# Attention with a planned order on TensorE: new planner constants, a longer lead, larger rings and masks in fp32r

## The chip, the cores and the metric

The kernel runs on one core of one Trainium2 chip. The time is that of the whole kernel on the device, in microseconds (us), as the median of three runs. A core has TensorE (PE, matmuls and weight loads), VectorE (DVE), ScalarE (ACT), GpSimd (POOL) and SyncE (SP, which issues the DMAs here). Each runs its own list of instructions in order, and they wait for each other by semaphores. Matmuls write to eight banks of PSUM, 512 fp32 columns each; DVE and ACT read them from there.

## What is computed

A transformer layer on x of shape (1, 4096, 256): a modulated layer norm, causal attention with 16 heads of 16 dimensions and rotary positions, a residual with a gate, a second norm, a dense layer, eight experts in fixed slices, a last dense layer, a second gated residual. The change touches the attention alone:

```python
scores = jnp.einsum('bhqd,bhkd->bhqk', q, k) * scale
mask = jnp.where(kpos > qpos, jnp.float32(-jnp.inf), jnp.float32(0.0))
scores = scores + mask[None, None]
attn = jax.nn.softmax(scores.astype(jnp.float32), axis=-1).astype(q.dtype)
out = jnp.einsum('bhqk,bhkd->bhqd', attn, v)
```

## The kernel before

The kernel has a projection stage (to about 140 us), the attention stage (`attend_block`, to about 1737 us) and a feed-forward stage (`feed`, to the end). Attention is cut into 32 tasks (`TASKS`): four quads of four heads, and in each quad eight chunks of 512 queries. A task with chunk c (0 to 7) sees c + 1 chunks of keys. `STEPS` are the blocks of 128 keys of each task, 4(c + 1) of them; the last four of a task lie on the diagonal, have 512, 384, 256 and 128 columns, and need the causal mask.

Scores are computed twice. The first time, `most` (lines 831 to 851), they stand with queries as rows, and DVE takes their maximum per row (line 940). `UNITS` lists this work, 8(c + 1) pairs of matmuls per task. When a task is through, DVE joins its maxima (line 946), POOL splits them into two fp32r parts (lines 979, 981), PE turns them (`turn`, line 859), ACT copies them out (line 917), and SP spreads them as extra rows of the queries (`spread`, line 764, by DMA from m_rows to q_aug). The second time, `scores` (line 817), the scores stand with keys as rows, the maximum is subtracted by those extra rows, and ACT takes the exponential (line 908). Then `values` (line 879) multiplies them with v into PSUM bank 3, in plain fp32. At a task's end ACT copies the result out (line 924), PE turns it (`norm`, line 867), and DVE divides by the row sums (lines 954, 956).

One `score` or `most` is a pair of fp32r matmuls that run side by side in the upper and lower 64 rows of the array (r = 0, 1), into two of the seven free banks. On the diagonal four small matmuls of 128 columns add the mask to the two banks (lines 825 and 849): id_h times later_h, both bf16, in two halves of 64 rows each.

What PE, ACT, DVE and SP do in which order is written out by `plan()` before the kernel is built. It keeps a clock for PE, ACT and DVE, and when each bank is free; at each turn it lists what could come next on PE (a score, a most, a turn, a norm, a values), reckons when each could begin (`begin_at`), and takes the one of least cost. The cost weighs how far ACT's or DVE's clock is ahead, biases, and PACE times the wait of PE. The constants below `plan()` say what each thing takes in its model. The model sets the order alone; on the chip semaphores decide when things run.

Limits on the order: a `most` of task n may be chosen only while n <= main + LEAD, where main is the task whose scores are next; its queries must have a slot in q_aug (QRING slots, freed when the scores of task n - QRING are done); its keys must have one of the KRING slots of k_aug (line 747; keys k beyond the first KRING wait until the scores of the last task of the quad of key k - KRING are done). Scores run at most PROBS = 4 blocks ahead of values.

SP's queue at the start of attention: keys 0 and queries 0, the two masks, a constant, queries 1 and keys 1, then 2 x KRING small writes of ones into the key slots (line 779), then the loads of the other slots, and only then what `SP_ORDER` lists: spreads, and reloads of queries and keys. The first `score` waits for the first spread, and for all writes of ones.

Of the kernel before, what the change touches and what calls it, by code (L numbers as in the profile page):

```python
# [25 lines left out]
P = 128  # L26
# [46 lines left out]
PV_BANK = 3  # L73
KRING = 12
QRING = 5
PROBS = 4
LEAD = 3


def step_width(s):  # L80
    n, kb = STEPS[s]
    return CW - P * max(kb - TILES * TASKS[n][1], 0)
# [16 lines left out]
def plan():  # L99

    pe_order, act_order, dve_order, sp_order = [], [], [], []
    pe = act = dve = 0.0
    wide = False
    free = {b: 0.0 for b in BANKS}
# [10 lines left out]

    def begin_at(ready, to_wide):
        if wide == to_wide and ready > pe - RELOAD:
            return max(pe + RELOAD, ready)
        return max(pe + (TO_VALUES if to_wide else FROM_VALUES if wide else 0), ready)

# [24 lines left out]
    while pair < pairs or val < len(STEPS) or at < len(UNITS) or turn or norm:  # L145
        choices = []
        main = STEPS[pair // JP][0] if pair < pairs else len(TASKS)
        if pair < pairs:
            s = pair // JP
            if main in rows and s - PROBS < val:  # L150
                banks, ready = take(2)
                begins = begin_at(max(ready, rows[main]), False)
                choices.append((act - begins + PACE * max(begins - pe, 0), "score", begins, banks))
        if at < len(UNITS):
            n = UNITS[at][0]
            if n <= main + LEAD and not (turn and late_nm is not None) and (n < QRING or n - QRING in main_end):
                banks, ready = take(2)
                begins = begin_at(max(ready, main_end[n - QRING] + LOAD_NS if n >= QRING else 0.0), False)
                choices.append((dve - begins + MOST_BIAS + PACE * max(begins - pe, 0), "most", begins, banks))
        for kind, small in (("turn", turn), ("norm", norm)):  # L160
            if small:
                banks, ready = take(1)
                begins = begin_at(max(ready, small[0]), False)
                choices.append((SMALL_BIAS + PACE * max(begins - pe, 0), kind, begins, banks))
        if val < pair // JP and not (norm and LAST[STEPS[val][0]] == val):
            begins = begin_at(max(exp_end[val], pv_free if STEPS[val][1] == 0 else 0.0), True)
            choices.append((VALUES_BIAS - VALUES_STEP * (pair // JP - val) + (VALUES_AGAIN if wide else 0)
                            + PACE * max(begins - pe, 0), "values", begins, None))
        _, kind, begins, banks = min(choices, key=lambda c: c[0])
        after = read_by(banks) if banks else None  # L170
        if kind == "score":
# [9 lines left out]
            if b == JP - 1 and LAST[main] == s:  # L181
# [3 lines left out]
                if s in LAST_OF_QUAD:  # L185
                    g = LAST_OF_QUAD.index(s)
                    for k in range(CHUNKS * g + KRING, min(CHUNKS * (g + 1) + KRING, CHUNKS * QUADS)):
                        sp_order.append((act, "keys", k))
            pair, pe, wide = pair + 1, begins + max(w * PE_COLUMN + PE_FIXED, PE_LEAST) + masks, False
        elif kind == "most":  # L190
# [9 lines left out]
            if at == LAST_UNIT[n]:  # L200
                if n == 0 or n == len(TASKS) - 1:
                    maxima_of(n)
                else:
                    late_nm = n
            at, pe, wide = at + 1, begins + max(w * PE_COLUMN + PE_FIXED, PE_LEAST) + masks, False
        elif kind == "turn":
            pe_order.append(("turn", turn[1], None, banks, after))
            pe, wide = begins + TURN_NS, False
            on_act(("turn", turn[1], None, banks[0]), pe + PE_TO_ACT, CW * ACT_COLUMN + ACT_FIXED, banks[0])
            rows[turn[1]] = act + SPREAD_NS  # L210
            sp_order.append((act, "spread", turn[1]))
            turn = None
        elif kind == "norm":
            pe_order.append(("norm", norm[1], None, banks, after))
            pe, wide = begins + TURN_NS, False
            on_dve(("norm", norm[1], None, banks[0]), pe + PE_TO_DVE, NORM_NS, banks[0])
            norm = None
        else:
            n = STEPS[val][0]
            pe_order.append(("values", val, None, None, None))  # L220
            pe, wide = begins + step_width(val) * PV_COLUMN, True
            pv_end[val] = pe
            if val == LAST[n]:
                on_act(("out", n, None, PV_BANK), pe + PE_TO_ACT, CW * ACT_COLUMN + ACT_FIXED, None)
                pv_free = act + ACT_TO_PE
                norm = (pv_free, n)
            val += 1
# [3 lines left out]
PE_COLUMN, PE_FIXED, PE_LEAST = 1 / 2.4, 22, 110  # L231
PV_COLUMN = 853 / 512
TO_VALUES, FROM_VALUES, RELOAD = 214, 114, 95
MASK_NS, TURN_NS = 125, 530
ACT_COLUMN, ACT_FIXED = 1 / 1.4, 112
DVE_COLUMN, DVE_FIXED = 1 / 0.96, 64
PE_TO_ACT, PE_TO_DVE, ACT_TO_PE, DVE_TO_PE = 312, 232, 164, 140
NM_NS, CUT_NS, NORM_NS, SPREAD_NS, LOAD_NS = 100, 1150, 700, 2400, 2600
PACE = 4.28
MOST_BIAS, SMALL_BIAS = -471, 627  # L240
VALUES_BIAS, VALUES_STEP, VALUES_AGAIN = 1100, 34, 1073

# [463 lines left out]
def attend_block(nc, sem, bank, ctx, a, v_all):  # L706
    def sb(name, shape, dt=F32):
        return ctx.enter_context(nc.sbuf_tensor(name, shape, dt))
# [4 lines left out]
    o_sb = sb("o_sb", [P, 2, CW])  # L713
    id_h = sb("id_h", [P, RTILES, P], BF16)
    later_h = sb("later_h", [P, RTILES, P], BF16)
    mx = sb("mx", [P, QRING, RTILES, JP, TILES, CHUNKS])
# [11 lines left out]
                                                            sem("norm_done"), sem("pv_done"))  # L728
    act_read, dve_read = sem("act_read"), sem("dve_read")
    nm_done, cut_done, linv_done = sem("nm_done"), sem("cut_done"), sem("linv_done")  # L730
    pv = bank(PV_BANK)
# [5 lines left out]
    with nc.Block() as block:  # L737
        @block.sync
        def _(sp):
# [29 lines left out]
            load_queries(0)  # L769
            sp.dma_start(id_h[:, :, :], a["halves"]).then_inc(masks_in, 16)  # L770
            sp.dma_start(later_h[:, :, :], a["later"]).then_inc(masks_in, 16)
            sp.dma_start(m_rows[0:MCOLS, :, :], a["ownrows"]).then_inc(ones_in, 16)
# [26 lines left out]
        def _(pe):  # L799
# [83 lines left out]

            pe.wait_ge(masks_in, 32)
            pe.wait_ge(pad_set, 1)
# [85 lines left out]
        @block.gpsimd  # L971
        def _(pool):
            nc.gpsimd.memset(nm_p[:, :, :].bitcast(F32), 0.0).then_inc(pad_set, 1)
            pool.wait_ge(pad_set, 1)
            for n in range(len(TASKS)):
                hi, lo = [nm_p[:, n % QRING, 0:TILES * RTILES * MCOLS]
                          .rearrange("p (t r n b) -> p n r b t", r=RTILES, n=PARTS, b=JP)[:, m] for m in range(PARTS)]
                pool.wait_ge(nm_done, n + 1)
                nc.gpsimd.tensor_copy(hi, nm[:, n % QRING, :, :, :]).then_inc(cut_done, 1)  # L979
                pool.wait_ge(cut_done, 2 * n + 1)  # L980
                nc.gpsimd.tensor_tensor(lo, nm[:, n % QRING, :, :, :], hi.bitcast(F32), ALU.subtract).then_inc(cut_done, 1)


# [595 lines left out]
def constants():  # L1579
    row = np.arange(RT)[:, None, None] + RT * np.arange(RTILES)[None, :, None]  # L1580
    col = np.arange(P)[None, None, :]
    later = np.where(row > col, np.float32(-1e30), np.float32(0))
    later, halves = (np.tile(m, (RTILES, 1, 1)).astype(mybir.dt.np(BF16)) for m in (later, row == col))
    own = np.tile(np.eye(JP, dtype=np.float32)[:, :, None], (PARTS, 1, CW))
# [45 lines left out]
```

## Time and profile before

| | |
|---|---|
| time, median of 3 runs | 2092.42 us (2088.43 to 2095.24) |
| profiled execution, own time | 2090.41 us |
| its span | 2088.6 us |
| PE busy | 1894.6 us (91%) |
| DVE busy | 1701.6 us (81%) |
| ACT busy | 1348.3 us (65%) |
| POOL busy | 236.6 us (11%) |
| granted clock of PE, mean | 0.949 |

The span runs from the first to the last instruction; the execution's own time has some 2 us around it. Busy time is the time in which at least one instruction of the engine runs; matmuls overlap, and their ends are modelled. The granted clock is the share of PE's full speed that the chip allowed.

### The profile page before, as it was taken

The numbers are of one execution on the slowest core, as the hardware profiler recorded it, in microseconds if no ns is written. First come the engines' busy times: TensorE is split into PE (matmuls) and PEld (weight loads), VectorE is DVE, ScalarE is ACT, GpSimd is POOL, SyncE is SP. The second block draws the span as 40 slices with busy tenths as digits, with TensorE's granted clock in tenths as the row PEclk, the third lists the DMA queues.
The fourth block names the chain that finished last, engine by engine and source line by source line (L and its number), as shares of the span: only waits on it lengthen the run. The fifth ranks groups of instructions, "written<-read, shape, count | busy, mean of one in ns | idle before, by whom it ended". The sixth has DMA issues, their size and how long they took to land. (4 is left out here: it accounts for less than half of the span.)

```text
span 2088.6 us, 36838 instructions
## 1 busy us (share of the span) xinstructions
PE 1894.6 (91%) x13224; PEld 888.2 (43%) x13224; DVE 1701.6 (81%) x2969; ACT 1348.3 (65%) x2675; POOL 236.6 (11%) x185
## 2 busy tenths in 40 slices
PE   7843899999999999999999999999999996869998
PEld 4521333333434433343433333344333324538887
DVE  5962899998959999996899999769999803978886
ACT  3411466677687777768777776787777793226553
POOL 4720000000000000000000000000000002544442
PEclk9965799999999999999999999999999998989999
DMA  5865000000003000000300000010000003203331
GB/s 179 226 165 112 10 9 9 9 8 2 10 2 86 10 9 9 10 10 2 85 10 9 10 9 9 3 55 9 2 2 2 1 2 137 70 11 109 106 112 34
DMA packets 58667, 86.90 MB, mean 42 GB/s; under 512 B 9412, under 2 KB 31428, under 8 KB 58504
## 3 DMA queue, kind: packets, MB, share of 16 engines
q1 hardware_dynamic: 58504, 84.70, 14.6%
q8 instruction: 106, 1.74, 0.3%
q14 instruction: 57, 0.47, 0.1%
HBM read 58.06 MB, written 20.97 MB: 38 GB/s over the span
## 5 line engine op out<-in xcount | busy, mean ns | idle before, releaser
L940 DVE TENSOR_REDUCE mx<-banks 128x1 f32<-128x512 f32 (+3 forms) x2304 | 1305.1, 638 | 202.3 <-PE banks L841 189.4
L908 ACT ACTIVATE prob<-banks 128x512 f32<-128x512 f32 (+3 forms) x2304 | 1116.8, 619 | 373.7 <-PE banks L817 267.1
L817 PE MATMUL banks<-q_aug,k_aug 52*128 52x512 f32 (+3 forms) x2304 | 532.7, 461 | 59.5 <-issue 26.1
L879 PE MATMUL banks<-prob,v_all 128*17 128x512 f32 (+3 forms) x4608 | 580.1, 576 | 0.0
L841 PE MATMUL banks<-k_aug,q_aug 48*128 48x512 f32 (+3 forms) x2304 | 518.7, 450 | 56.7 <-DMA later_h<-in_later 26.1
L817 PEld LDWEIGHTS banks<-q_aug,k_aug 52*128 52x128 f32 x2304 | 227.7, 188 | 493.1 <-ACT prob L908 306.6
L841 PEld LDWEIGHTS banks<-k_aug,q_aug 48*128 48x128 f32 x2304 | 233.5, 190 | 306.8 <-ACT prob L908 193.1
L979 POOL CAST nm_p<-nm 128x16 fp32r<-128x16 f32 x32 | 6.8, 214 | 1510.0 <-DVE nm L946 1510.0
L879 PEld LDWEIGHTS banks<-prob,v_all 128*17 128x17 f32 x4608 | 77.0, 96 | 164.9 <-issue 86.9
L849 PE MATMUL banks<-id_h,later_h 64*128 64x128 bf16 x1024 | 77.5, 228 | 0.0
L825 PE MATMUL banks<-later_h,id_h 64*128 64x128 bf16 x1024 | 76.0, 225 | 0.0
L1508 DVE TENSOR_TENSOR hid_lo<-hid,hid_hi 128x512 fp32r<-128x512 f32 x64 | 56.7, 912 | 21.7 <-ACT hid_hi L1446 20.7
L917 ACT ACTIVATE m_rows<-banks 8x512 f32<-8x512 f32 x32 | 18.6, 581 | 77.9 <-DMA k_aug<-m_rows 39.8
L954 DVE RECIPROCAL l_inv<-banks 128x16 f32<-128x16 f32 x32 | 7.9, 248 | 67.8 <-PE banks L867 67.8
L669 PE MATMUL banks<-hT,w_qk 128*128 128x512 f32 x128 | 58.0, 607 | 1.9 <-ACT hT L595 1.9
L1163 ACT ACTIVATE x3T<-banks,ln_col 128x512 f32<-128x512 f32 x16 | 12.0, 776 | 72.6 <-PE banks L1096 72.5
L447 POOL TENSOR_TENSOR rest<-qk,cs 128x1024 f32<-128x1024 f32 x16 | 53.6, 3374 | 31.1 <-ACT qk L605 31.1
L1446 ACT ACTIVATE w_hi<-w_s 128x1024 fp32r<-128x1024 f32 x28 | 28.0, 1051 | 41.9 <-PE banks L1337 41.9
L1337 PE MATMUL banks<-xe_hi,w_hi 128*128 128x512 f32 x128 | 50.7, 396 | 3.2 <-DVE xe_lo L1499 3.2
L1337 PE MATMUL banks<-hid_lo,w_hi 128*128 128x512 f32 x128 | 51.0, 398 | 0.0
L1209 DVE TENSOR_SCALAR xn<-h,mv,rstd 128x256 f32<-128x256 f32 x32 | 47.5, 1543 | 4.2 <-POOL rstd L1263 4.2
L1337 PE MATMUL banks<-xe_lo,w_hi 128*128 128x512 f32 x128 | 50.8, 397 | 0.0
(113 smaller groups left out, 1471.6 us busy)
## 6 DMA issues: line engine op xcount, KB each, us to landing
parts_scratch<-p SPq DMA_DIRECT2D x64, 256.0 KB, 4.1
w_s<-in_w SPq DMA_DIRECT2D x16, 1024.0 KB, 5.5
xs<-in_x SPq DMA_DIRECT2D x16, 512.0 KB, 4.6
k_aug<-parts_scratch SPq DMA_DIRECT2D x64, 128.0 KB, 3.2
q_aug<-parts_scratch SPq DMA_DIRECT2D x64, 128.0 KB, 2.6
cs<-in_rope SPq DMA_DIRECT2D x8, 512.0 KB, 5.8
k_aug<-parts_scratch SPq DMA_DIRECT2D x64, 64.0 KB, 3.1
q_aug<-parts_scratch SPq DMA_DIRECT2D x64, 64.0 KB, 2.6
```

The source lines that it names most:

```text
L447: nc.gpsimd.tensor_tensor(rest[:, par, eo, :, :], qk[:, eo, :, :], cs[:, par, 1:2, :].broadcast_to([P, 2, CW]), ALU.mult)\
L669: mm = nc.tensor.matmul(bank(QK_BANKS + 2 * eo + b), w_qk[:, h, eo, b, :], hT[:, off % 2, h, :], start=(h == 0), stop=(h == HALF - 1))
L817: mm = nc.tensor.matmul(bank(banks[r])[:, q0:CW], keys[rows], q_aug[rows, n % QRING, b, q0:CW], start=True, stop=True)
L825: mm = nc.tensor.matmul(bank(banks[r])[:, q0:q0 + P], id_h[tile, half, :], later_h[tile, half, :], start=False, stop=True, skip_group_chec ...
L841: mm = nc.tensor.matmul(bank(banks[r])[:, 0:width], q_aug[rows, n % QRING, b, t * P:(t + 1) * P], k_aug[rows, b, key_slot(n, kc)[0], 0:wid ...
L849: mm = nc.tensor.matmul(bank(banks[r])[:, t * P:width], later_h[tile, half, :], id_h[tile, half, :], start=False, stop=True, skip_group_ch ...
L879: mm = nc.tensor.matmul(pv[32 * j:32 * j + VW, q0:CW], v_all[:, g, kb, j, :], prob[:, s % PROBS, j, q0:CW], start=(kb == 0), stop=(s == LA ...
L908: nc.scalar.activation(prob[:, s % PROBS, j, q0:CW], bank(from_bank)[:, q0:CW], ACT.Exp, scale=float(HD) ** -0.5).then_inc(act_read, 1)
L940: nc.vector.tensor_reduce(mx[:, n % QRING, r, b, t, kc:kc + 1], bank(from_bank)[:, 0:unit_width(i)], AX_X, ALU.max).then_inc(dve_read, 1)
L1209: nc.vector.tensor_scalar(xn[:, k, par, t, :], src(t), mv[:, k, par, t, 0:1], rstd[:, k, par, t:t + 1], ALU.subtract, ALU.mult).then_inc(x ...
L1337: mm = nc.tensor.matmul(out, lhs(p), rhs(q), start=start and n == 0, stop=stop and n == len(PASSES) - 1)
L1508: nc.vector.tensor_tensor(hid_p[1][:, k, :], hid[:, k % HB, :], hid_p[0][:, k, :].bitcast(F32), ALU.subtract).then_inc(h_lo, 1)
```

## The change

- LEAD goes from 3 to 4, QRING from 5 to 6, KRING from 12 to 14.
- In `plan()` the flag `wide` becomes a `mode` (pair, values, turn). A change of mode costs a drain of the old one and the weight load of the new one; a pair after a pair begins at the later of PE's clock and 107 ns after its banks are free. Turns and norms are a mode of their own. All constants of durations, latencies and biases are set anew, among them MASK_NS from 125 to 214 and TURN_NS from 530 to 436.
- The masks become fp32r. They come as fp32 by DMA into o_sb, and two copies on POOL write them to id_h and later_h as fp32r; PE's first wait is for these copies.
- `cut(n)` on POOL is a function now; what it does is the same.

```diff
-KRING = 12
-QRING = 5
+KRING = 14
+QRING = 6
 PROBS = 4
-LEAD = 3
+LEAD = 4
...
-    def begin_at(ready, to_wide):
-        if wide == to_wide and ready > pe - RELOAD:
-            return max(pe + RELOAD, ready)
-        return max(pe + (TO_VALUES if to_wide else FROM_VALUES if wide else 0), ready)
+    def begin_at(ready, to):
+        if mode == to == "pair":
+            return max(pe, ready + WEIGHTS["pair"])
+        return max(pe + (0 if mode == to else DRAIN[mode]), ready) + (0 if mode == to else WEIGHTS[to])
...
-PV_COLUMN = 853 / 512
-TO_VALUES, FROM_VALUES, RELOAD = 214, 114, 95
-MASK_NS, TURN_NS = 125, 530
+PV_COLUMN = 1.667
+WEIGHTS = {"pair": 107, "values": 15, "turn": 15}
+DRAIN = {"pair": 85, "values": 115, "turn": 93}
+MASK_NS, TURN_NS = 214, 436
 ACT_COLUMN, ACT_FIXED = 1 / 1.4, 112
-DVE_COLUMN, DVE_FIXED = 1 / 0.96, 64
-PE_TO_ACT, PE_TO_DVE, ACT_TO_PE, DVE_TO_PE = 312, 232, 164, 140
+DVE_COLUMN, DVE_FIXED = 1 / 0.96, 65
+PE_TO_ACT, PE_TO_DVE, ACT_TO_PE, DVE_TO_PE = 212, 212, 168, 135
 NM_NS, CUT_NS, NORM_NS, SPREAD_NS, LOAD_NS = 100, 1150, 700, 2400, 2600
-PACE = 4.28
-MOST_BIAS, SMALL_BIAS = -471, 627
-VALUES_BIAS, VALUES_STEP, VALUES_AGAIN = 1100, 34, 1073
+PACE = 4.56
+MOST_BIAS, SMALL_BIAS = -224.94, 1260.31
+VALUES_BIAS, VALUES_STEP, VALUES_AGAIN = 1557.84, 72.31, 2180.34
...
-    id_h = sb("id_h", [P, RTILES, P], BF16)
-    later_h = sb("later_h", [P, RTILES, P], BF16)
+    id_h = sb("id_h", [P, RTILES, P], F32R)
+    later_h = sb("later_h", [P, RTILES, P], F32R)
...
-            sp.dma_start(id_h[:, :, :], a["halves"]).then_inc(masks_in, 16)
-            sp.dma_start(later_h[:, :, :], a["later"]).then_inc(masks_in, 16)
+            sp.dma_start(o_sb[:, 0, 0:RTILES * P], a["halves"].rearrange("p h c -> p (h c)")).then_inc(masks_in, 16)
+            sp.dma_start(o_sb[:, 1, 0:RTILES * P], a["later"].rearrange("p h c -> p (h c)")).then_inc(masks_in, 16)
...
-            pe.wait_ge(masks_in, 32)
+            pe.wait_ge(masks_cut, 2)
...
+            pool.wait_ge(masks_in, 32)
+            nc.gpsimd.tensor_copy(id_h[:, :, :].rearrange("p h c -> p (h c)"), o_sb[:, 0, 0:RTILES * P])\
+                .then_inc(masks_cut, 1)
+            nc.gpsimd.tensor_copy(later_h[:, :, :].rearrange("p h c -> p (h c)"), o_sb[:, 1, 0:RTILES * P])\
+                .then_inc(masks_cut, 1)
```

## Rows read from the trace of the kernel before

**Rows 1.** The page's busy time by engine, share of the span and instructions

```profile
PE 1894.6 (91%) x13224; PEld 888.2 (43%) x13224; DVE 1701.6 (81%) x2969; ACT 1348.3 (65%) x2675; POOL 236.6 (11%) x185
```

**Rows 2.** Busy time by stretch (us): stretch, length, engines, PE's granted clock, DMA

```profile
195.00:603.00 408.00, 381.93 (x2786) 153.30 (x2788) 366.56 (x667) 260.90 (x532) 4.05 (x18) 0.90 0.03 9
603.00:630.00 27.00, 27.00 (x214) 8.01 (x214) 0.19 (x1) 26.62 (x59) 0.00 (x0) 1.00 0.01 2
630.00:975.00 345.00, 335.22 (x2676) 136.18 (x2672) 330.59 (x600) 261.03 (x537) 3.60 (x16) 1.00 0.08 20
195.00:1668.00 1473.00, 1419.64 (x11012) 564.80 (x11012) 1309.04 (x2367) 1083.53 (x2236) 13.49 (x60) 0.97 0.06 15
1668.00:1737.00 69.00, 64.88 (x448) 18.65 (x444) 1.14 (x4) 62.36 (x131) 0.45 (x2) 0.95 0.01 2
```

**Rows 3.** Timeline of DVE: start, duration, engine, line, what, [idle before, its releaser]

```profile
595.10 8.10 DVE L940 TENSOR_REDUCE mx<-banks 128x1 f32<-128x512 f32 x18 [0.30 <-PE banks L841]
630.34 1.29 DVE L940 TENSOR_REDUCE mx<-banks 128x1 f32<-128x512 f32 x2 [27.15 <-PE banks L841]
...
1001.01 1.29 DVE L940 TENSOR_REDUCE mx<-banks 128x1 f32<-128x512 f32 x2 [26.12 <-PE banks L841]
...
1376.09 1.29 DVE L940 TENSOR_REDUCE mx<-banks 128x1 f32<-128x512 f32 x2 [26.13 <-PE banks L841]
```

**Rows 4.** Waits between 199 and 1668: who for whom, us, times, longest

```profile
DVE mx L940 <- PE banks L841: 154.1, 180, 27.2
...
ACT prob L908 <- PE banks L825: 73.2, 122, 1.5
```

**Rows 5.** Timeline in the middle of a quad, one period of the order

```profile
1500.62 0.50 PE L841 MATMUL banks<-k_aug,q_aug 48*128 48x512 f32 x2
...
1500.96 0.40 PE L817 MATMUL banks<-q_aug,k_aug 52*128 52x512 f32 x2
...
1501.19 0.40 PE L841 MATMUL banks<-k_aug,q_aug 48*128 48x512 f32 x2
...
1501.52 1.05 PE L879 MATMUL banks<-prob,v_all 128*17 128x512 f32 x8
...
1502.50 0.50 PE L817 MATMUL banks<-q_aug,k_aug 52*128 52x512 f32 x2
...
1505.80 0.50 PE L841 MATMUL banks<-k_aug,q_aug 48*128 48x512 f32 x2
...
1506.33 4.88 DVE L940 TENSOR_REDUCE mx<-banks 128x1 f32<-128x512 f32 x8 [0.30 <-PE banks L841]
```

**Rows 6.** Timeline of SP's queue as the third quad begins

```profile
1002.52 17.27 SPq L747 DMA_DIRECT2D k_aug<-parts_scratch  x32
```

**Rows 7.** Timeline at the start of attention, SP's queue and PE's first score

```profile
149.48 16.49 SPq L779 DMA_DIRECT2D k_aug<-m_rows  x24
...
175.68 14.92 SPq L747 DMA_DIRECT2D k_aug<-parts_scratch  x32
190.64 1.36 SPq L764 DMA_DIRECT2D q_aug<-m_rows  x2
...
195.30 0.79 PE L817 MATMUL banks<-q_aug,k_aug 52*128 52x512 f32 x2 [26.11 <-issue]
```

**Rows 8.** The page's groups of instructions: POOL's row of 1024 columns (busy, mean ns)

```profile
L447 POOL TENSOR_TENSOR rest<-qk,cs 128x1024 f32<-128x1024 f32 x16 | 53.6, 3374 | 31.1 <-ACT qk L605 31.1
```

**Rows 9.** Timeline on the diagonal: bf16 masks and a pair of 128 columns

```profile
326.14 0.12 PEld L825 LDWEIGHTS banks<-later_h,id_h 64*128 64x128 bf16 x4
326.14 0.29 PE L825 MATMUL banks<-later_h,id_h 64*128 64x128 bf16 x4
326.21 0.19 PEld L841 LDWEIGHTS banks<-k_aug,q_aug 48*128 48x128 f32 x2
326.24 0.31 PE L841 MATMUL banks<-k_aug,q_aug 48*128 48x128 f32 x2
...
326.39 0.29 PE L849 MATMUL banks<-id_h,later_h 64*128 64x128 bf16 x4
```

## What the change was predicted to do

> **What bounds the kernel now.** I read four views, in this order. First the page's busy shares: TensorE (PE) is shown busy for 91% of the span and VectorE (DVE) for 81% [rows 1]. PE's share misleads, since the ends of its matmuls are modelled. So I went on to the busy time by stretch [rows 2]. Between 195 and 1668 us, where everything that the change touches runs, DVE is busy for 1309 of 1473 us. A quad's end has almost none of it: from 603 to 630 DVE works 0.19 us, and ScalarE (ACT) 26.6 of 27. Outside that DVE is at 90% in the first quad and at 96% from 630 to 975.
>
> The timeline shows three such holes and what ends them: DVE was idle for 27.15, 26.12 and 26.13 us, released each time by PE's matmul of line 841, a block of scores that is made only for its row maxima ("most" in the order, M here) [rows 3]. Together 79.4 us. They lie in the last task of a quad, and end as the first task of the next begins. The list of waits puts all of DVE's waiting for line 841 between 199 and 1668 at 154.1 us [rows 4], so the holes are half of it; the other 177 waits are some 0.4 us each.
>
> Then one period in the middle of a quad [rows 5], of 5.18 us (1500.62 to 1505.80) for two key blocks: four M, four score pairs (S) and two value products (V). DVE's eight reductions take 4.88, after a wait of 0.30 (1506.33). PE's own need for one key block, with no bank waited for, is V up to the next pair 0.98 (1501.52 to 1502.50), the pair after it 0.34 (as 1500.62 to 1500.96), then two pairs at 0.23 (1500.96 to 1501.19) and the last pair up to V 0.33 (1501.19 to 1501.52): 2.11 us against 2.44 for DVE's four reductions and 2.59 taken. So DVE sets the pace, PE has some 19% to spare, and ACT more. That ends with the last M: from 1668 on DVE has 1.1 us of work and the last task's S and V run out on ACT and PE until 1737 [rows 2].
>
> **The lead: LEAD 3 to 4, with rings of six and fourteen.** M of task n may be put in only while n is at most the task of S plus LEAD. The tasks of a quad need 8, 16, ... 64 M pairs. While S is in the last task of a quad, M can be ahead by the next quad's first LEAD tasks: 8 + 16 + 24 = 48 pairs with 3, 80 with 4. But the 64 M pairs of that last task must all be done before its S begins, and in step (one M for one S) the lead of 64 would stay 64. So with 3 at least 16 pairs of lead must be given up, at 1.22 us of DVE each 20 us of hole, and with the latency from a maximum to its row in the queries the 26 seen. With 4 the allowance of 80 is above 64, and nothing is given up. DVE's work is fixed, S of the last task needs the last M, and the tail after that is as before; so each microsecond of hole filled is one off the span. S runs slower in the filled stretch, since in the hole it has PE and ACT to itself (ACT 26.6 of 27 us [rows 2]), but those M pairs are then missing later. The six query slots let task n+4 load two tasks ahead, as five did for n+3, and fourteen key slots hold six key chunks of the next quad at its end where twelve hold four, and LEAD 4 needs chunks 0 to 3 there: no load is late. The eight key loads that SP still has to issue at a quad's end (32 DMAs, 17.27 us [rows 6]) stay in front of the next spread; with M one task further ahead that spread is for a task whose S comes later, so this cover grows. Sum: -79, bounds -79 (all) and -50 (if PE, below, holds a third back).
>
> **The start.** S of task 0 waits for the spread of its maxima, which stands in SP's queue behind the loads of the rings: 24 writes of ones took 16.49 us (0.687 each, to 165.97), then query and key loads up to 190.64, where the first spread goes out, and PE begins S at 195.30 [rows 7]. From 165.97 to 190.64 that is 24.67 us for 3 query and 10 key loads, 1.90 each. The change adds 4 writes of ones (2.75) and one query and two key loads (5.69): +8.4 us, while PE and DVE stand idle already, so all of it is on the path. If the new order puts more M into the hole it costs less: bounds 0 and 9.
>
> The masks reach PE through two copies on GpSimd of 256 columns, at most 0.9 us each by its row of 1024 columns at 3.37 [rows 8]. Twice that delays the first M, and is hidden: ACT's first turn waits for all writes of ones, which SP issues up to 165.97 [rows 7]. Without that cover it would cost at most 2 us. Masks of twice the bytes, the larger fill of nm_p and the added semaphore cost nothing for the same reason.
>
> **The masks in fp32r.** There are 32 tasks x 4 diagonal key blocks x 2 pairs = 256 mask groups for S, and as many for M. In bf16 a group takes 0.10 us of PE (326.14 to 326.24) [rows 9]. As fp32r it becomes two pairs of 128 columns; the nearest row, M's own 128 columns between masks, takes 0.15 from its start to the next (326.24 to 326.39 [rows 9]). Twice that is 0.30, the upper end. The lower end is the array's time alone, two quarters of a pair of 512 columns at 0.23 [rows 5], 0.115. I take the middle, 0.21: +0.11 a group, 56 us of PE in all, bounds 8 and 102. The M half falls where PE has room. In the S half PE is already late: ACT waits 73.2 us for the masks of line 825 [rows 4]. So I put the S half alone on the path: 256 x 0.11 = +28 us, bounds 0 and 102.
>
> Here a rule speaks against the change. The trace has four bf16 weight loads in 0.12 us and two fp32r ones in 0.19 [rows 9]. The Trainium skill, "TensorE: Matmul & The Clock Gate", section "Weight-path perf modes — Fast Weight Load (FWL) and DoubleRow", says that the quick load is for 128 weights of a type that isn't FP32; the trace agrees. By the Trainium skill, under the same title, section "LDWEIGHTS (loading the stationary operand)", a load of 128 columns takes 107 ns, so the four of a group would cost 0.43, an estimate by that section, and the S half 256 x 0.33 = 84 us instead of 28.
>
> **The order.** New constants sort all of S, M, V and the transposes anew. What that does to the short waits can't be read from before. Outside the holes DVE idles 1473 - 1309 - 79.4 = 85 us: 41.4 of 408 us in the first quad (10.1%), 14.4 of 345 in the second (4.2%) [rows 2], the remaining 29 later. With the first quad at the second's rate 24 are saved (41.4 - 17.1); with all later ones at the first's (986 us x 10.1% = 100, less the 43 that they have) 57 are lost. I take 0.
>
> **The sum.** The profiled execution took 2090.4 us (span 2088.6), 2 us under the median of 2092.4. -79 + 8 + 28 + 0 = -43: 2047 us. Nothing after the attention stage changes. The granted clock is 0.90 over the first quad and 1.00 over the second [rows 2], between the levels of 1.2 and 2.4 GHz; PE's wait ahead of it is longer but not of another kind, so I give that no term.
>
> **The rivals.**
> (a) The holes close and the new order is tighter too: -79 + 8 + 28 - 24 to -79 + 8 + 0 - 24, 2023 to 1995. For it: DVE at 96% in one stretch shows that such an order exists. Against: fuller stretches leave PE less room.
> (b) PE takes DVE's place, on the other side. Place: the diagonal key blocks of S and M. Price: both halves of the masks on the path at 0.30, +102 against -71 from holes and start: +31, 2121. It decides from an extra of 71 / 512 = 0.139 us a group; below that it only eats the gain. For it: PE at 2.11 of DVE's 2.44 a block has no room for 8 masks in 4 blocks on top. Against: each wait of DVE in the diagonals is small now, 18 reductions in one piece [rows 3].
> (c) The fp32r weight loads don't hide: two take 0.19 [rows 9], a group 0.38, extra 0.28; S half alone 72 us, 2091; both halves 143, 2163. By the Trainium skill's formula above, in "TensorE: Matmul & The Clock Gate", it would go this way. Against it: the pair of 128 columns with its two loads took 0.15, less than the loads alone, so they overlap.
> (d) The change doesn't do what it says: the planner may put M into the last task and yet hold it back for another cause (a bank, PACE, the order of the small turns), and the holes stay. Then 2090 + 8 + 28 = 2127. Against: each M after a hole comes with the very start of the next quad's first S (630.34, 1001.01, 1376.09), as the limit and nothing else would have it.
>
> **How the numbers follow.** Forecast 0.52, own range 2025 to 2080; (a) 0.18; (b) 0.16, of which 0.03 still faster, 0.05 the same, 0.08 slower; (c) 0.05, of which 0.01 the same; (d) 0.06, slower; 0.03 for what I don't see, 0.01 the same and 0.02 slower. Within 0.3% (6 us) is about what this measurement can't tell from no change. Faster 0.52 + 0.18 + 0.03 = 0.73; same 0.07; slower 0.08 + 0.04 + 0.06 + 0.02 = 0.20. The range 2000 to 2105 leaves out (d), most of (c), the worst third of (b) and the edge of (a), under 0.2.
>
> **What would show it.** Right: no DVE wait over 10 us between 200 and the last reduction; first S at 203 to 204; mask groups at 0.2 to 0.3; the last M some 40 us earlier, the tail after it still near 69 us. Wrong: DVE holes of 20 us or more at the quads' ends (d); short waits of DVE for lines 841 and 849 above 130 us in sum, most beside masks (b, c); or key blocks in mid-quad longer than 2.6 us, which would be the order itself.

## The result, and the profile after

The changed kernel takes 2077.05 us (median of 7 runs, 2068.85 to 2082.45) against 2092.1 for the kernel before (median of 7, 2088.43 to 2095.24): a ratio of 0.9926 [0.9908, 0.9944], 15.5 us less. The forecast was 43 less. The direction held and the time lies in the range; about a third of the gain came.

The profiled execution of after took 2082.45 us (span 2080.7), the longest of its seven and 5 us above their median. Where single numbers of its trace are set against other kernels, a difference of that size carries no weight.

The page's busy time by engine, as in [rows 1]:

```profile
PE 1893.3 (91%) x13224; PEld 961.4 (46%) x13224; DVE 1711.1 (82%) x2969; ACT 1347.8 (65%) x2675; POOL 237.4 (11%) x187
```

PE and DVE have the instructions that they had, and their busy time is the same to within 10 us; weight loads (PEld) have 73 us more than in [rows 1], with masks of twice the bytes. Busy time by stretch, after, with the columns of [rows 2] (stretch, length, PE, PEld, DVE, ACT, POOL, PE's granted clock, DMA share, GB/s):

```profile
206.00:606.00 400.00, 371.54 (x2704) 166.77 (x2701) 356.25 (x644) 253.59 (x521) 4.03 (x18) 0.90 0.03 9
606.00:660.00 54.00, 53.73 (x477) 27.23 (x470) 50.21 (x96) 41.70 (x90) 0.90 (x4) 1.00 0.11 32
660.00:1005.00 345.00, 341.19 (x2687) 148.13 (x2685) 323.45 (x579) 274.19 (x557) 3.15 (x14) 1.00 0.05 16
206.00:1650.00 1444.00, 1403.80 (x10888) 627.18 (x10887) 1318.25 (x2367) 1071.06 (x2206) 13.49 (x60) 0.96 0.05 14
1650.00:1725.00 75.00, 73.79 (x566) 23.89 (x562) 0.94 (x3) 73.34 (x160) 0.45 (x2) 1.00 0.01 1
```

The quad's end has filled: DVE works 50.2 of the 54 us around it (606 to 660), where [rows 2] had 0.19 of 27. But ACT is down to 41.7 of 54, where it had 26.6 of 27; that is the first sign of what the filling cost: S runs slower there. The timeline of DVE, after, in the form of [rows 3]:

```profile
1020.12 1.29 DVE L942 TENSOR_REDUCE mx<-banks 128x1 f32<-128x512 f32 x2 [5.87 <-PE banks L843]
...
1385.89 1.29 DVE L942 TENSOR_REDUCE mx<-banks 128x1 f32<-128x512 f32 x2 [7.13 <-PE banks L843]
...
1649.97 0.29 DVE L948 TENSOR_REDUCE nm<-mx 128x16 f32<-128x128 f32 x1
1670.01 0.26 DVE L956 RECIPROCAL l_inv<-banks 128x16 f32<-128x16 f32 x1 [19.75 <-PE banks L869]
```

Of the three holes of [rows 3], 79.4 us in all, rests of 5.87 and 7.13 are left at two quads' ends and none at the first. M's work ends at 1649.97. Then DVE is idle for 19.75 us until the division of the task before the last (1670.01). In before that wait was 3.55 us:

```profile
1671.51 0.26 DVE L954 RECIPROCAL l_inv<-banks 128x16 f32<-128x16 f32 x1 [3.55 <-PE banks L867]
```

So M is through some 13 us before the exponentials of the task before the last are (1649.9 against 1662.8), and no longer holds up the end. The waits between 210 and 1650, after (who for whom, us, times, longest), in the form of [rows 4]:

```profile
PEld banks L819 <- ACT prob L910: 251.5, 407, 1.2
ACT prob L910 <- PE banks L819: 230.7, 364, 3.9
PEld banks L843 <- ACT prob L910: 203.6, 375, 1.7
DVE mx L942 <- PE banks L843: 94.0, 185, 7.1
ACT prob L910 <- PE banks L827: 78.2, 110, 3.4
```

DVE's waits for M fell from 154.1 to 94.0. PE and ACT wait for each other: the weight loads of S (line 819) and of M (line 843) stand before the exponentials' banks for 251.5 and 203.6 us, and the exponentials before S for 230.7. That is nothing new: in before the same three waits, between 199 and 1668, were 271.7, 193.1 and 263.8. The start, after, in the form of [rows 7]:

```profile
149.44 0.40 POOL L978 CAST id_h<-o_sb 128x256 fp32r<-128x256 f32 x1 [6.90 <-DMA o_sb<-in_later]
...
150.36 19.20 SPq L781 DMA_DIRECT2D k_aug<-m_rows  x28
...
183.42 16.79 SPq L749 DMA_DIRECT2D k_aug<-parts_scratch  x36
200.26 1.36 SPq L766 DMA_DIRECT2D q_aug<-m_rows  x2
...
205.52 0.80 PE L819 MATMUL banks<-q_aug,k_aug 52*128 52x512 f32 x2 [32.72 <-issue]
```

A mask's copy on POOL takes 0.40 us (the estimate from [rows 8] was 0.9 at most). The first spread goes out at 200.26 instead of 190.64, and S begins at 205.52 instead of 195.30. The masks, after, in the form of [rows 9]:

```profile
337.49 0.49 PE L819 MATMUL banks<-q_aug,k_aug 52*128 52x512 f32 x2
337.60 0.42 PEld L827 LDWEIGHTS banks<-later_h,id_h 64*128 64x128 f32 x4
337.82 0.34 PE L827 MATMUL banks<-later_h,id_h 64*128 64x128 f32 x4
...
338.00 0.48 PE L843 MATMUL banks<-k_aug,q_aug 48*128 48x512 f32 x2
```

A mask group takes 0.18 us from its start to the next matmul (337.82 to 338.00), where it took 0.10 [rows 9]. Its four weight loads stand for 0.42 us, but begin 0.22 ahead of the group, while the pair of 512 columns (337.49) still runs.

### The profile page after: what moved, and what is told of

It is laid out like the page before. It is cut to its first block and busy times, and to the rows that moved or that the text cites. A ratio compares the mean times of both kernels' runs of the same rounds, so it can differ in the third digit from the quotient of the medians.

```text
span 2080.7 us, 36982 instructions
## 1 busy us (share of the span) xinstructions
PE 1893.3 (91%) x13224; PEld 961.4 (46%) x13224; DVE 1711.1 (82%) x2969; ACT 1347.8 (65%) x2675; POOL 237.4 (11%) x187
## 5 line engine op out<-in xcount | busy, mean ns | idle before, releaser
L819 PE MATMUL banks<-q_aug,k_aug 52*128 52x512 f32 (+3 forms) x2304 | 524.9, 452 | 51.5 <-issue 32.7
L843 PEld LDWEIGHTS banks<-k_aug,q_aug 48*128 48x128 f32 x2304 | 234.4, 192 | 314.7 <-ACT prob L910 203.6
L851 PEld LDWEIGHTS banks<-id_h,later_h 64*128 64x128 f32 x1024 | 97.8, 200 | 3.1
L851 PE MATMUL banks<-id_h,later_h 64*128 64x128 f32 x1024 | 97.2, 264 | 0.0
L827 PEld LDWEIGHTS banks<-later_h,id_h 64*128 64x128 f32 x1024 | 93.4, 196 | 5.8
L827 PE MATMUL banks<-later_h,id_h 64*128 64x128 f32 x1024 | 94.0, 261 | 0.0
```

Of the source, the lines that this page charges most:

```text
L819: mm = nc.tensor.matmul(bank(banks[r])[:, q0:CW], keys[rows], q_aug[rows, n % QRING, b, q0:CW], start=True, stop=True)
L827: mm = nc.tensor.matmul(bank(banks[r])[:, q0:q0 + P], id_h[tile, half, :], later_h[tile, half, :], start=False, stop=True, skip_group_chec ...
L843: mm = nc.tensor.matmul(bank(banks[r])[:, 0:width], q_aug[rows, n % QRING, b, t * P:(t + 1) * P], k_aug[rows, b, key_slot(n, kc)[0], 0:wid ...
L851: mm = nc.tensor.matmul(bank(banks[r])[:, t * P:width], later_h[tile, half, :], id_h[tile, half, :], start=False, stop=True, skip_group_ch ...
```

## A sum that holds for every kernel here

What an idle microsecond of an engine is worth can't be read from the engine itself. So I cut the attention stage by the exponentials on ACT's timeline, which end every score block, into three terms: when the first one begins; the time inside the 32 tasks (a task's first exponential to the end of its last); and the 31 changes of task between (end of a task's last exponential to the first of the next). Their sum is the end of the last exponential. What follows it took 353 to 358 us in all kernels here.

| kernel | first | inside | between | last ends | between, by quad |
|---|---|---|---|---|---|
| before | 196.3 | 1423.0 | 115.2 | 1734.6 | 65.9, 16.9, 17.0, 15.4 |
| after | 206.6 | 1399.4 | 118.5 | 1724.5 | 85.1, 14.1, 11.5, 7.8 |
| b_plan | 198.3 | 1362.4 | 191.3 | 1752.0 | 81.5, 37.0, 36.9, 35.9 |
| b_lead4 | 205.7 | 1428.9 | 94.4 | 1729.0 | 66.6, 10.0, 10.7, 7.2 |
| b_fp32r | 196.3 | 1429.9 | 119.6 | 1745.8 | |
| a_bf16 | 206.0 | 1384.0 | 112.4 | 1702.4 | 81.1, 12.8, 10.6, 8.0 |
| a_lead3 | 207.7 | 1371.0 | 190.3 | 1769.0 | 81.8, 36.6, 36.5, 35.4 |
| a_cap70 | 205.3 | 1405.9 | 108.8 | 1720.1 | 83.0, 8.3, 8.3, 9.2 |
| a_holes10 | 205.9 | 1382.9 | 154.9 | 1743.6 | 81.5, 24.8, 24.8, 23.8 |
| a_dve_half | 206.0 | 1359.4 | 115.8 | 1681.3 | |
| a_v_half | 206.0 | 1350.4 | 117.3 | 1673.7 | |
| a_va_half | 206.4 | 1315.2 | 123.2 | 1644.9 | |
| best | 175.4 | 1383.4 | 112.8 | 1671.6 | |

The reductions of M (DVE's, two for a pair, 2304 in all) can be counted the same way, by where they start. In every kernel 28 come before the first exponential. Inside the tasks, beside S, start 2088 in before, 2095 in after, 1971 in b_plan, 2120 in b_lead4, 2094 in a_bf16 and 2032 in a_holes10; the rest run in the changes of task.

Names with b_ are the kernel before with one part of the change; names with a_ are the kernel after with one part undone or altered. Below, a ratio stands against the kernel before, run beside it; times 2092 us it gives the microseconds that are named.

## The experiments

### The new order alone (b_plan)

```diff
-    def begin_at(ready, to_wide):
...
+    def begin_at(ready, to):
...
-PACE = 4.28
-MOST_BIAS, SMALL_BIAS = -471, 627
...
+PACE = 4.56
+MOST_BIAS, SMALL_BIAS = -224.94, 1260.31
...
```

That is the kernel before with `mode` and all new constants, but LEAD 3, rings of five and twelve, and bf16 masks.

> The kernel before with the planner's new mode rule and constants alone: LEAD 3, rings of 5 and 12, bf16 masks. Worked out from the runs so far: the changed kernel with LEAD 3 took 2125, of which the masks are 15 to 17 and the longer start 9, so 2100, 11 over before: the new constants order worse where the lead is 3. My prediction's term of 0 says 2089; theory 'a tighter order' says under 2080.

2110.09 us, 1.0081 [1.0064, 1.0098]: 17 us slower, more than the 11 worked out beforehand. By the table the order makes the tasks 60.6 us shorter inside and the changes of task 76.1 longer. A change of task shows where. b_plan, timeline, from the last exponential of task 14 to the first of task 15:

```profile
923.08 0.45 ACT L909 ACTIVATE prob<-banks 128x128 f32<-128x128 f32 x2 [0.23 <-PE banks L826]
...
928.18 0.27 DVE L947 TENSOR_REDUCE nm<-mx 128x16 f32<-128x128 f32 x1
...
930.49 0.59 ACT L918 ACTIVATE m_rows<-banks 8x512 f32<-8x512 f32 x1 [6.97 <-PE banks L860]
...
931.10 1.35 SPq L765 DMA_DIRECT2D q_aug<-m_rows  x2
```

The exponentials of task 14 end at 923.53. Task 15's maxima are joined at 928.18, 4.7 us later; the turn and the spread follow, and the first exponential of task 15 comes at 934.71: 11.2 us in which no score can be made. The scores have caught up with the maxima, and a lead of three tasks doesn't hold them apart. The order that `plan()` writes out shows it too: four M pairs of task 15 stand behind the last score pair of task 14, where before has none.

### LEAD 4 and the rings alone (b_lead4)

```diff
-KRING = 12
-QRING = 5
+KRING = 14
+QRING = 6
...
-LEAD = 3
+LEAD = 4
```

> The kernel before with LEAD 4 and rings of 6 and 14, its old planner constants and bf16 masks. My prediction's step: -79 + 8 (longer start) = 2021. Theory 'lead only moved': the holes are gone but the span falls by 10 to 35 us only, 2060 to 2080, with VectorE idle again before the last task. Theory 'order' (the new constants cost what the lead gave): like the prediction's step, 2020 to 2035.

2086.3 us, 0.9983 [0.9972, 0.9994]: 3.6 us faster, where the forecast had -71 for LEAD and start together. b_lead4, timeline of DVE:

```profile
1017.97 1.29 DVE L940 TENSOR_REDUCE mx<-banks 128x1 f32<-128x512 f32 x2 [20.07 <-PE banks L841]
...
1388.21 1.29 DVE L940 TENSOR_REDUCE mx<-banks 128x1 f32<-128x512 f32 x2 [20.08 <-PE banks L841]
...
1671.78 0.26 DVE L954 RECIPROCAL l_inv<-banks 128x16 f32<-128x16 f32 x1 [26.92 <-PE banks L867]
```

The hole of the first quad is gone, but those of the second and third are there, shorter by 6 us each. The limit LEAD still makes them: by the order of `plan()` M is 98 pairs ahead at the first score of tasks 15 and 23, where before has 73, and is held until the lead is down to 81 at the last (49 in before). And DVE stands idle for 26.92 us once M is through, against 3.55 in before. Of 79.4 us of holes 39 were closed, and the span fell by 3.6. In the old order M was far enough ahead with LEAD 3: its changes of task in the later quads cost 15 to 17 us a quad, and there was little to win. The start costs 9.4 us, where 8.4 was forecast.

### After with LEAD 3 (a_lead3)

```diff
-LEAD = 4
+LEAD = 3
```

> The changed kernel with LEAD back at 3; rings, constants and fp32r masks stay. My prediction's step (each microsecond of hole filled is one off the span): the three holes of 26 us come back in place of 13 us in two rests, so about 66 us more, 2143. Theory 'lead only moved' (scores and values on TensorE are late too, so the holes filled come back as short waits and as waiting at the end): 10 to 35 us more, 2090 to 2110. Theory 'masks' says nothing of it.

2125.14 us, 1.0176 [1.0159, 1.0192]: 52 us over after. The changes of task take 190.3, as in b_plan, against 118.5; inside the tasks it is 28.4 faster. So LEAD is worth 52 in the new order, and in the old one, with its rings, 3.6, or 13 without the start's 9.4. The fall in the three later quads is alike: from 35 to 37 us a quad to 8 to 14.

### After with bf16 masks (a_bf16), before with fp32r masks (b_fp32r)

```diff
-    id_h = sb("id_h", [P, RTILES, P], F32R)
-    later_h = sb("later_h", [P, RTILES, P], F32R)
+    id_h = sb("id_h", [P, RTILES, P], BF16)
+    later_h = sb("later_h", [P, RTILES, P], BF16)
...
```

The second is the same edit the other way round, in the kernel before; the two copies on POOL and their semaphore go with the masks.

> The changed kernel in every instruction of its order, with the masks back in bf16. In the two traces a mask group takes 0.095 us of TensorE in bf16 and 0.172 in fp32r (shortest start to start), 0.077 x 512 = 39 us in all. Theory 'masks' (they ate the gain): 39 us less if all is on the path, 2038, and 20 less if half is, 2057; VectorE's short waits fall back by as much. Theories 'order' and 'lead only moved': the time stays near 2077, since the order and the lead stay.

> The kernel before, its order unchanged, with the masks in fp32r alone. Theory 'masks': 39 us more if all is on the path, 2131; 20 more if half is, 2112; the prediction had 28 more, 2120. If the masks hide behind VectorE: 2092, no change.

a_bf16: 2060.05 us, 0.9866 [0.9849, 0.9882]. b_fp32r: 2103.87 us, 1.006 [1.004, 1.008]. In either order fp32r masks cost 0.006, 12.6 us, give or take 5. The shortest distance from a mask group's start to the next matmul is 0.095 us in bf16 and 0.171 to 0.173 in fp32r: 0.077 more. But only 152 of the 512 bf16 groups of before are followed within 0.11 us. Over all groups the mean distance, waits included, rises from 0.211 (before) to 0.257 (b_fp32r) and from 0.213 (a_bf16) to 0.263 (after), which is 24 to 26 us for 512 groups; half of that reaches the span. a_bf16 against b_plan is LEAD with the rings and the start in the new order: 0.9866 - 1.0081, 45 us. At the change of task of which b_plan's rows stand above, a_bf16's timeline has:

```profile
909.22 0.27 DVE L947 TENSOR_REDUCE nm<-mx 128x16 f32<-128x128 f32 x1
...
918.42 1.37 ACT L909 ACTIVATE prob<-banks 128x256 f32<-128x256 f32 x6 [0.65 <-PE banks L826]
920.73 0.59 ACT L918 ACTIVATE m_rows<-banks 8x512 f32<-8x512 f32 x1 [0.94 <-PE banks L860]
922.14 2.07 ACT L909 ACTIVATE prob<-banks 128x512 f32<-128x512 f32 x4 [0.83 <-PE banks L818]
```

Task 15's maxima are joined at 909.22, 10.6 us before task 14's exponentials end (918.42 + 1.37 = 919.79), and task 15's begin 2.4 us after, instead of 11.2.

### Is it the lead itself (a_cap70)

```diff
-            if n <= main + LEAD and not (turn and late_nm is not None) and ...
+            if n <= main + LEAD and at - pair < 70 and not (turn and late_nm is not None) and ...
```

> The changed kernel, in whose planner a most pair may also be put in only while fewer than 70 most pairs are ahead of the score pairs (before the cap the lead at the quads' ends is 73, 77 and 87). Theory 'lead only moved' (VectorE works ahead of need and the scores come late): no hole over 6 us in VectorE, the last maxima later, the wait after them shorter by some 10 us, and the span 5 to 20 less, 2057 to 2072. If work ahead is free, as my prediction has it: 2077 or more.

2077.6 us, 0.9933 [0.9911, 0.9954]: no change, though after lets M run 71 to 90 pairs ahead in the second and third quads and here it stops at 70. So the last pairs of lead are worth nothing, and holding M back gains nothing either.

### After with the holes made again (a_holes10)

```diff
+            barred = pair < pairs and main % CHUNKS == CHUNKS - 1 and pair // JP > LAST[main] - 10
-            if n <= main + LEAD and not (turn and ...
+            if n <= main + LEAD and not barred and not (turn and ...
```

M may not run beside the last ten key blocks of a quad.

> The changed kernel, in whose planner no most pair may be put in during the last ten key blocks of a quad's last task. That makes three holes in VectorE of some 18 us (ten blocks at 1.85 us), and the lead over the score pairs still stays above what each later task needs (at least 54 and 73 before the last task). My prediction's step (a microsecond of hole is one on the span): 55 more, 2132. Theory 'the score stream sets the pace, and a most pair costs it the same wherever it stands' (blocks take 1.9 us without and some 2.6 with two most pairs, so 0.34 a pair): no change, 2067 to 2087.

2105.92 us, 1.0082 [1.0058, 1.0106]: 33 us over after, between the two theories, so neither had it. Its timeline of DVE at the first quad's end:

```profile
637.73 2.48 DVE L943 TENSOR_REDUCE mx<-banks 128x1 f32<-128x512 f32 x4 [17.64 <-PE banks L844]
```

There is one such hole of 17.6 us at each of the three ends, 53 us in all. Time inside the tasks falls by 16.5 us: with 63 reductions fewer beside it S is faster. The changes of task rise by 36.4; the lead at a quad's start is 55 pairs where after has 74 to 82. (The table gives 19 for the sum and the ratios 33, since the profiled run of a_holes10 was the shortest of its four, 2098.39, and that of after the longest of its seven.) So the price of a hole shows not in its quad's last task but later: in a_holes10 the changes into the first six tasks of the next quad cost at most 2.1 us each, and those into its last two 7 and 10, where after has at most 3.4. That it depends on the lead, and is nothing with 70 pairs at a quad's start (a_cap70) but not with 55, fits both runs; no value between was run.

### Does DVE set the pace (a_dve_half, a_v_half, a_va_half)

```diff
-  bank(from_bank)[:, 0:unit_width(i)], AX_X,
+  bank(from_bank)[:, 0:unit_width(i) // 2], AX_X,
```

```diff
+                q1 = (q0 + CW) // 2 if kb else CW
-                    mm = nc.tensor.matmul(pv[32 * j:32 * j + VW, q0:CW], v_all[:, g, kb, j, :],
+                    mm = nc.tensor.matmul(pv[32 * j:32 * j + VW, q0:q1], v_all[:, g, kb, j, :],
```

The third has the second edit and the exponentials cut in the same way.

> The changed kernel with each row maximum taken over half the columns (the other half is left out); order and TensorE's work unchanged. VectorE's work falls by some 0.27 us x 2304 x 0.9 = 560 us. If VectorE sets the pace, as my prediction has it, the span falls until TensorE's need of 2.11 of 2.59 us a key block stops it: 150 us or more, under 1930. If TensorE's order with ScalarE's reads sets it, the span falls by under 60, above 2015.

> The changed kernel with the value products over half their columns except in a task's first key block (the other half is left out); order and VectorE's work unchanged. TensorE's work falls by some 0.41 us x 544 = 220 us. If VectorE sets the pace: under 40 less, above 2035. If TensorE is the late one: 100 or more, under 1980.

> The changed kernel with value products and exponentials over half their columns except in a task's first key block (the other half is left out); order and VectorE's work unchanged. With the values halved alone it took 2031. Theory 'score stream': TensorE and ScalarE wait for each other round the banks, so with both shorter the time falls well below that, under 1960, until VectorE's 1310 us plus start and tail bind. If VectorE sets the pace: 2010 to 2031.

One run each, with the order of every engine left as it was: 2036.47, 2030.59 and 2003.09 us, which is 41, 46 and 74 under after's median (its own runs lie within 9 us of that). The first is what was expected if PE's order with ACT's reads sets the pace; the other two fall between their theories. Busy time up to the last M, first a_dve_half:

```profile
206.00:1605.00 1399.00, 1355.22 (x10881) 602.18 (x10880) 812.04 (x2366) 1065.80 (x2205) 13.40 (x60) 0.97 0.05 14
```

then a_v_half:

```profile
206.00:1598.00 1392.00, 1323.37 (x10889) 685.69 (x10892) 1299.81 (x2367) 1073.72 (x2207) 13.38 (x60) 0.92 0.05 14
```

and a_va_half:

```profile
206.00:1593.00 1387.00, 1316.66 (x10894) 686.06 (x10894) 1298.83 (x2367) 720.33 (x2208) 13.37 (x60) 0.92 0.06 15
```

DVE's work falls from 1318 to 812 us and the span by 41, 8% of the 506 us. An engine that sets the pace would have given most of it back. Here DVE waits for M instead, between 210 and 1640 for 495.9 us where after has 94.0. a_dve_half, list of waits:

```profile
DVE mx L942 <- PE banks L843: 495.9, 648, 7.6
```

ACT's work falls by 353 us from the second to the third kernel, and the span by 27. So in this order no single engine sets the pace. The granted clock, between its levels of 1.2 and 2.4 GHz, was 0.92 in the two kernels with fewer columns of V, against 0.96 to 0.97, so their gain may be understated.

The Trainium skill, "Perfetto Trace Analysis", section "Identifying the Most-Contended Engine", says that the engine with the highest occupancy is the most contended one and is to be optimized first, with the warning that PE's own busy time misleads. By that rule DVE, at 91% of 206 to 1650, is first. The measurement doesn't bear it out here: 506 us of DVE's work were worth 41.

### A version that beats both (best, best2)

```diff
+            spread(0)
             for n in range(2, QRING):
                 load_queries(n)
                 load_keys(n)
+            spread(1)
             for k in range(QRING, KRING):
                 load_keys(k)
             for kind, n in SP_ORDER:
+                if kind == "spread" and n < 2:
+                    continue
```

This is in a_bf16: the first spread goes out behind the ones, ahead of the loads that fill the rings. best2 also puts the ones in 4 larger writes instead of 28.

> The changed kernel with bf16 masks and with the first spread ahead of the loads of the rings on SyncE's queue, the second spread ahead of key loads 6 to 13; the order on TensorE is unchanged. The first score waits from 172 to 205 in the changed kernel; 16 loads at 1.9 us no longer stand before its spread: 30 less than the 2060 with bf16 masks, 2030, if all of the wait is on the path. If the first quad is held by its maxima in any case: 2050 to 2060.

> As the run with the first spread moved, and the 28 small writes of ones as 4 larger ones. They took 0.687 us each on the queue, 19 us ahead of the first turn's copy: 10 to 15 less again, 2015 to 2020, if the landing of the larger writes takes some 4 us; if the writes themselves take as long in one piece, no change.

best: 2030.55 us, 0.9715 [0.9699, 0.9732]; best2: 2031.59 us, 0.9717 [0.9701, 0.9733]. best, timeline at the start:

```profile
149.81 19.20 SPq L780 DMA_DIRECT2D k_aug<-m_rows  x28
...
170.67 0.59 ACT L922 ACTIVATE m_rows<-banks 8x512 f32<-8x512 f32 x1 [42.42 <-DMA k_aug<-m_rows]
171.28 1.32 SPq L765 DMA_DIRECT2D q_aug<-m_rows  x2
...
175.40 2.97 ACT L913 ACTIVATE prob<-banks 128x512 f32<-128x512 f32 x6 [4.14 <-PE banks L830]
```

The first exponential comes at 175.4 instead of 206.0, and the other two terms of the table stay: 30.6 us there, 31.6 by the ratios. What stood on the path at the start was worth twice what the whole change brought. best2, same view:

```profile
150.41 9.44 SPq L780 DMA_DIRECT2D k_aug<-m_rows  x4
...
170.16 0.59 ACT L923 ACTIVATE m_rows<-banks 8x512 f32<-8x512 f32 x1 [41.31 <-DMA k_aug<-m_rows]
170.77 1.32 SPq L765 DMA_DIRECT2D q_aug<-m_rows  x2
```

The writes are issued in half the time, by 159.85, but ACT's first turn, which waits for them to land, comes at 170.16 against 170.67, the spread follows at 170.77 against 171.28, and nothing is won.

## Why the prediction was right in direction and wrong in size

The measured parts, in the order in which they were added: order +17, LEAD with rings and start -45, masks +12.6, together -15.5. The forecast had 0, -71 and +28: the misses are +17, +26 and -15.

**What bounds the kernel: the step that failed.** "So DVE sets the pace", read from 96% in a stretch [rows 2] and from one period [rows 5], and from it "each microsecond of hole filled is one off the span". The holes did close, from 79.4 us to 13.0. But 506 us less of DVE's work gave 41 (a_dve_half). The list of waits of before, from which [rows 4] comes, spoke against it (between 199 and 1668):

```profile
PEld banks L817 <- ACT prob L908: 271.7, 436, 1.5
...
PEld banks L841 <- ACT prob L908: 193.1, 374, 1.7
...
PEld banks L817 <- DVE mx L940: 41.2, 75, 0.9
...
PEld banks L841 <- DVE mx L940: 13.0, 33, 0.9
```

PE's weight loads for S and M waited 464.8 us for banks that ACT was reading, and 54.2 for those that DVE was reading. (Matmuls run beside some of these waits, so they rank the two and don't price them.) Another row stood in the prediction and was read as a side matter: in the hole ACT worked 26.62 of 27 us, and from 630 to 975 only 261 of 345 [rows 2]. By ACT's work S ran at 0.986 against 0.757, 1.30 times as fast; 79.4 us of hole were worth about 24 us to the score stream (79.4 x 0.30). Filling the holes takes that back. b_plan has three holes of 23.1 us and a_bf16 one rest of 6.7, 62.6 less (x 0.30 = 19); time inside the tasks rises by 21.6 between them. a_holes10 has 53 where after has 13 (40 x 0.30 = 12), and gains 16.5. From before to b_lead4 39 are closed (12), and 5.9 came, so the estimate is good to a factor of two. The count of reductions fits no worse: a_bf16 has 123 more beside S than b_plan, 0.18 us each (21.6 / 123); b_lead4 has 32 more than before (32 x 0.18 = 5.8, and 5.9 came), a_holes10 63 fewer than after (11, and 16.5 came). It also says why closing the holes brought nothing by itself: before and after have as many reductions beside S (2088 and 2095). "But those M pairs are then missing later" was right, and is why a hole is not a loss.

**The lead.** What a longer lead gives is that a task's maxima are there when the task before ends. In the old order that was nearly always so, and LEAD 4 is worth 3.6 with the start's 9.4 us in it (b_lead4). There "in step (one M for one S) the lead of 64 would stay 64" failed too: in the later quads M runs up to 98 pairs ahead before the last task, and a limit of 80 makes holes again. In the new order it takes 78.9 us out of the changes of task (191.3 to 112.4). That this nearly equals the 79 of the forecast is luck: the place and the mechanism are others. The term should have been read from the waits of S at each change of task: 49 us in the three later quads of before, of which LEAD 4 alone took 21.

**The order.** I took 0 with bounds of -24 and +57. Alone it costs 17 us: 60.6 gained inside the tasks, 76.1 lost between. With LEAD 4 and the start in both it gains 24 (a_bf16 0.9866 against b_lead4 0.9983). What it gains shows inside the tasks: with as many reductions beside S (2094 and 2088) they take 39.0 us less in a_bf16 than in before. The parts aren't separable, and a sum that costs each against the kernel before, as mine did, can't show that. It was on DVE's idle time that I bounded it, which is not where it acts: DVE's waits for the M line without the holes went up, from 74.7 (154.1 less 79.4) to 81.0 (94.0 less 13.0), and with the mask line from 77.5 to 101.1.

**The masks.** The direction held, the size was too large: 0.171 us a group at the shortest, not 0.21, and 12.6 us, not 28. The added 0.11 a group was 0.046 to 0.050 in the mean, and 256 of that would be 12 to 13; that it is the S half that lies on the path no run shows. Rival (c), loads that don't hide, is out: in the group shown the four take 0.42 us, half of it ahead of the group. By the Trainium skill, "TensorE: Matmul & The Clock Gate", section "LDWEIGHTS (loading the stationary operand)", the four loads would take 0.43 us, an estimate by its formula. The trace has 0.42 in that group and a median of 0.37 over the 512 groups. Where the prediction worked out 84 us by this rule, all masks cost 12.6: the loads overlap the pair before.

**The start.** +8.4 was forecast, +9.4 to +10.3 came (b_lead4, after): the ones and loads as counted, and S began at 205.52, not 203 to 204. The copies on POOL were hidden: the writes of ones end later (169.56).

**The signs named beforehand.** No wait of DVE over 10 us: so. Short waits for M and masks above 130 us, the sign of (b) and (c): no, 101.1. Key blocks in mid-quad longer than 2.6 us: no, the median in the fourth to sixth tasks of the quads is 2.57, as in before. So no sign of being wrong came. But the last M, which was to come 40 us earlier, came 17.7 earlier (1667.6 to 1649.9), and the tail from there to the last exponential grew from 67.0 to 74.6 instead of staying. That is the sign which should have overthrown the reading at once: the first exponential of the last task came 6.0 us after the last M before, and 13.9 after it now, as S was still in task 30. "S of the last task needs the last M" was true, but M was no longer what came last.

**The rivals.** (d) is out. (a) was half there: the holes close and the order is tighter, but inside the tasks and not in DVE's waits, and LEAD 3 would have lost it again. (b) is out: its price was 102 us for the masks, and they cost 12.6.

**What stays open.** The changes of task in the first quad cost 81 us in the new order and 66 in the old one, whatever LEAD is. The written orders show where: from task 2 to 7 four M pairs of a task stand behind the last score pair of the one before, where the old order has one. So its maxima are joined 5.46 us after the last exponential (a_bf16) instead of 2.61 (before), and as much later at each of these six changes; why the new constants place them so was not looked into. Open is also why the new order is faster inside the tasks, and what bounds the time there: halving the work of DVE, or of V, or of V and ACT, each gave a part. That PE and ACT hold each other up through the banks, each in its written order, fits the waits shown above, but was argued and not isolated.

## What to carry to other kernels

A busy share of 96% in a stretch doesn't show that an engine sets the pace; ask whose reads PE's bank waits end on, and what another engine does in that one's idle time, and if it speeds up there, count the difference only. Between two loops that run side by side with a lead, cost the lead where the follower waits for it, at each handover, and cost a new order and a new lead together. Before the steady state is tuned, look at what the first step waits for in a queue: here one moved transfer was worth 30 us.

## What the hardware showed that was not expected

- Four fp32r mask matmuls of 128 columns take 0.171 us to the next matmul at the shortest, where four bf16 ones take 0.095, although their weight loads stand for 0.42 us in the rows shown: half of that lies beside the pair ahead of them.
- The granted clock, between its levels of 1.2 and 2.4 GHz, was 0.96 over the stretch in after, and 0.92 in the two kernels with half the columns of V. These are one run each, and no run isolates the cause.
- 28 writes of ones occupy SP's queue for 19.20 us, and 4 writes of the same bytes for 9.44, but the turn that waits for them came no earlier (the spread at 171.28 and 170.77).
